# One continuous GpSimd gather stream beside seventeen stages, with a counted meeting of the other four engines

## What is computed

```python
x = x + L0_conv(group_norm(x))          # q, k, v by 1x1 and depthwise 3x3; 9 sampled points per pixel and group
t = layer_norm(tokens(x))
t = tokens(x) + t + attention(t)        # 1-D convolutions of width 3 give q, k, v; 8 heads, 4096 x 4096 softmax
t = t + mixture_of_experts(layer_norm(t))
```

## Time and profile before

| | |
|---|---|
| time, 3 runs | 9876.05, 9892.16, 9906.31 us (median 9892.16) |
| the profiled execution | 9916.45 us, its span 9914.7 us |
| mean granted TensorE clock | 0.884 |
| sampling stages | from 518.6 to 7860.9 us |
| first and last gather | 524.7 and 7385.7 us |

### The profile page before, as it was taken

One profiled execution on the slowest core, in us unless ns is written; L12 is line 12 of the kernel. 1 busy time (PEld: TensorE's weight loads), 2 busy tenths in 40 slices (PEclk: granted clock), 3 DMA queues, 4 the chain that ended last, 5 costly groups with the idle time before them and its releaser, 6 DMA issues. The chain is left out here.

```text
span 9914.7 us, 96863 instructions
## 1 busy us (share of the span) xinstructions
PE 7715.1 (78%) x31522; PEld 4163.2 (42%) x31522; DVE 5176.9 (52%) x10029; ACT 3769.7 (38%) x5495; POOL 5070.3 (51%) x4864
## 2 busy tenths in 40 slices
PE   7736665643796499977999967886999699998698
PEld 3623332443343244433444433443444344444466
DVE  6543334554565466655666645664663266644233
ACT  2101102300363166634666523562566245551222
POOL 1066776566677667776777767676750000001222
PEclk9868887876798699987999979898999899998899
DMA  3844335575553544444454454545441311106221
GB/s 127 296 138 129 120 118 159 184 233 190 155 148 104 167 130 136 133 149 131 141 147 136 124 157 153 154 136 158 138 123 40 94 31 45 47 20 172 87 71 55
DMA packets 658548, 1283.60 MB, mean 129 GB/s; under 512 B 189044, under 2 KB 398219, under 8 KB 643409
## 3 DMA queue, kind: packets, MB, share of 16 engines
q0 software_dynamic: 234240, 639.57, 21.5%
q1 hardware_dynamic: 405392, 562.58, 19.2%
q10 hardware_dynamic: 18432, 75.51, 1.9%
HBM read 1003.44 MB, written 278.91 MB: 129 GB/s over the span
## 5 line engine op out<-in xcount | busy, mean ns | idle before, releaser
L666 POOL DMA_INDIRECT sa_slot<-s_table,sa_rec x4608 | 4811.9, 1044 | 2540.8 <-issue 1374.5
L1657 DVE CUSTOM_DVE_ANT_0 a_above<-a_late,a_above 128x512 f32<-128x512 f32 x1600 | 1102.5, 689 | 1430.9 <-PE a_late L1509 1323.3
L1589 ACT ACTIVATE a_p<-a_s 128x1024 f32<-128x1024 f32 x1600 | 1628.0, 1020 | 124.0 <-PE a_s L1547 122.2
L1564 PE MATMUL a_ctx<-a_p,a_v 128*64 128x512 f32 x6400 | 1572.6, 612 | 85.1 <-issue 84.6
L1598 ACT ACTIVATE a_above<-a_diff 128x512 f32<-128x512 f32 x1600 | 957.7, 599 | 1780.9 <-PE a_diff L1497 1515.1
L713 DVE TENSOR_TENSOR sa_slot<-sa_slot,sa_q 128x1152 f32<-128x1152 f32 x512 | 694.0, 1355 | 1059.0 <-DMA sa_slot<-s_table,sa_rec 1041.4
L1547 PE MATMUL a_s<-a_q,a_k 98*128 98x512 f32 x3200 | 1047.0, 411 | 4.2 <-ACT a_p L1589 4.2
L822 PE MATMUL sa_sums<-keep_ident,sa_vals 128*128 128x128 f32 x4608 | 674.3, 295 | 453.9 <-DVE sa_vals L765 453.9
L1497 PE MATMUL a_diff<-a_kd,a_q 96*128 96x512 f32 x1600 | 724.9, 453 | 338.6 <-DMA a_q<-s_q 301.7
L1509 PE MATMUL a_late<-a_k,a_q 96*128 96x512 f32 x1600 | 816.0, 510 | 167.7 <-DVE a_pair_max L1657 166.1
L822 PEld LDWEIGHTS sa_sums<-keep_ident,sa_vals 128*128 128x128 f32 x4608 | 603.1, 154 | 551.8 <-DVE sa_vals L765 472.6
(11 more groups left out here) (280 smaller groups left out, 8093.8 us busy)
## 6 DMA issues: line engine op xcount, KB each, us to landing
sa_slot<-s_table,sa_rec POOLq DMA_INDIRECT x4608, 3.1
s_table<-t_rows ACTq DMA_DIRECT2D x64, 1024.0 KB, 8.0
a_q<-s_q SPq DMA_DIRECT2D x480, 128.0 KB, 3.5
s_part<-a_o SPq DMA_DIRECT2D x160, 256.0 KB, 2.4
t_qwin<-s_dwq SPq DMA_DIRECT2D x64, 512.0 KB
t_kvwin<-s_dwkv SPq DMA_DIRECT2D x64, 386.0 KB, 8.7
a_kd<-s_kd SPq DMA_DIRECT2D x384, 64.0 KB
a_o<-s_part SPq DMA_DIRECT2D x96, 256.0 KB, 3.3
```

The source lines that it names most:

```text
L666: pool.indirect_dma_start(out=self.slot[g][:, k, :, :, :].rearrange("p c a n -> p (c a n)"), out_offset=None, in_=self.s["table"][n // TIL ...
L1564: mm = pe.matmul(self.ps_ctx[i * 2 * HD:(i + 1) * 2 * HD, :], self.v_and_ones(run.head, kb), self.p[slot % P_SLOTS][:, i * CHUNK:(i + 1) * ...
L1589: act.activation(self.p[slot % P_SLOTS][:, :], self.ps_s[slot % 2], ACT.Exp, scale=float(HD) ** -0.5).then_inc(self.exped, 1)
L1657: dve.tensor_tensor_reduce(above, self.ps_late, above, 1.0, LOWEST, ALU.add, ALU.max, self.pair_max[:, t, j:j + 1]).then_inc(self.late_got, 1)
```

## The change

A new `Flow` opens one block around all stages with sampling. Inside it a stage is a `FlowStage`: it has no block and no barrier of its own; at its end TensorE, ScalarE, VectorE and SP drain, add 1 each to one semaphore and wait until it has reached four times the number of ended stages. SP then clears the stage's semaphores. POOL takes no part: all 4608 gathers are written as one program, limited by `tile_in`, `values_made` and the landing waits alone; before tile 32 it waits for the meeting at the end of `stage_tables_ahead`. The target rule (`freed`, the `todo` list) is gone. In `stage_maps_ahead` SP waits for each chunk of the convolution by itself and does its sampling work up to that chunk's target in between. Targets, buffers and the other engines' work are unchanged.

```diff
+class Flow(Stage):
+    ENGINES = 4
+
+    def __init__(self, nc):
+        super().__init__(nc)
+        self.met = nc.alloc_semaphore(name="flow_met")
+        self.sems.append(self.met)
+        self.block = self.enter_context(nc.Block())
+        self.ended = 0
+
+    def meeting(self):
+        return self.ENGINES * self.ended
+
+class FlowStage(ExitStack):
...
+    def meet(self):
+        flow, block = self.flow, self.flow.block
+        flow.ended += 1
+        numbers = sorted(sem.num for sem in self.sems)
+
+        @block.tensor
+        def _(pe):
+            pe.drain().then_inc(flow.met, 1)
+            pe.wait_ge(flow.met, flow.meeting())
...
+        @block.sync
+        def _(sp):
+            sp.drain().then_inc(flow.met, 1)
+            sp.wait_ge(flow.met, flow.meeting())
+            for _, same in groupby(enumerate(numbers), lambda item: item[1] - item[0]):
+                row = [number for _, number in same]
+                sp.sem_clear(range(row[0], row[-1] + 1))
+
+        for sem in self.sems:
+            self.nc.release_semaphore(sem)
...
-    def pool(self, pool, target):
-
-        todo = [j for j in range(self.done["POOL"], B * TILES * G) if self.freed(j) + HALF <= target]
-        for j in todo:
-            self.gather(pool, j // G, j % G)
-        self.done["POOL"] += len(todo)
...
+    def pool(self, pool, flow, tables_met):
+        for n in range(B * TILES):
+            if n == TILES:
+                pool.wait_ge(flow.met, tables_met)
+            for g in range(G):
+                self.gather(pool, n, g)
...
             for m in range(MT):
-                sp.wait_ge(conv_got, CHUNKS * (m + 1))
+                for c in range(CHUNKS):
+                    sp.wait_ge(conv_got, CHUNKS * m + c + 1)
+                    if c < CHUNKS - 1:
+                        sa.sync(sp, pieces(m, c))
...
-        @block.gpsimd
-        def _(pool):
-            sa.pool(pool, upto)
...
-def stage_project(nc, d, s, keep, b, c, sa, begin, upto):
+def stage_project(flow, d, s, keep, b, c, sa, begin, upto):
...
-    with Stage(nc) as stack:
+    nc, block = flow.nc, flow.block
+    with FlowStage(flow) as stack:
...
+                with Flow(nc) as flow:
+                    done = sa.stored_at(OWN_BLOCKS)
+                    stage_maps_ahead(flow, d, s, keep, 1, sa, done)
+                    for b in range(B):
+                        for c in range(QBS):
+                            if (b, c) == (0, 1):
+                                begin, done = done, sa.stored_at(2 * OWN_BLOCKS)
+                                stage_tables_ahead(flow, d, s, keep, 1, sa, begin, done)
+                                tables_met = flow.meeting()
...
+                            stage_project(flow, d, s, keep, b, c, sa, begin, done)
+                            if (b, c) < (B - 1, QBS - 1):
+                                done = stage_attention(nc, d, s, keep, b, c, row_max, sa, done, flow)
+
+                    @flow.block.gpsimd
+                    def _(pool):
+                        sa.pool(pool, flow, tables_met)
```

More of the change, by code:

```diff
@@ L1 @@
 from contextlib import ExitStack
+from itertools import groupby
 import concourse.bass as bass
@@ L76, in __exit__, with __init__, _ @@
             self.nc.all_engine_barrier()
+class Flow(Stage):
[9 more added lines that the diff above has]
+class FlowStage(ExitStack):
+    def __init__(self, flow):
+        super().__init__()
+        self.flow, self.nc, self.sems = flow, flow.nc, []
+    def __exit__(self, *error):
+        super().__exit__(*error)
+        if error[0] is None:
+            self.meet()
+    def meet(self):
[6 more added lines that the diff above has]
+            pe.wait_ge(flow.met, flow.meeting())
+        @block.scalar
+        def _(act):
+            act.drain().then_inc(flow.met, 1)
+            act.wait_ge(flow.met, flow.meeting())
+        @block.vector
+        def _(dve):
+            dve.drain().then_inc(flow.met, 1)
+            dve.wait_ge(flow.met, flow.meeting())
+        @block.sync
[7 more added lines that the diff above has]
+            self.nc.release_semaphore(sem)
 class Room:
@@ L603, in __init__ @@
         self.links = 0
-        self.done = {"SP": 0, "PE": 0, "ACT": 0, "DVE": 0, "POOL": 0}
+        self.done = {"SP": 0, "PE": 0, "ACT": 0, "DVE": 0}
     def turn(self, engine, target):
@@ L670, in gather @@
             ).then_inc(self.gathered[g] if k < EARLY else self.gathered_late[g], 16)
-    def pool(self, pool, target):
-        todo = [j for j in range(self.done["POOL"], B * TILES * G) if self.freed(j) + HALF <= target]
-        for j in todo:
-            self.gather(pool, j // G, j % G)
-        self.done["POOL"] += len(todo)
-    def freed(self, j):
-        n, g = divmod(j, G)
-        return self.PIECES * (n - 1) + HALF * (g // 4) + 11 + g % 4
+    def pool(self, pool, flow, tables_met):
[4 more added lines that the diff above has]
+                self.gather(pool, n, g)
     def vector(self, dve, target):
@@ L833, in project, with stage_maps_ahead @@
         mm.then_inc(self.projected, 1)
-def stage_maps_ahead(nc, d, s, keep, b, sa, upto):
-    with Stage(nc) as stack:
+def stage_maps_ahead(flow, d, s, keep, b, sa, upto):
+    nc, block = flow.nc, flow.block
+    with FlowStage(flow) as stack:
         r = Room(nc, stack, "n")
@@ L861, in stage_maps_ahead @@
         conv_mm, conv_got, diag_made, edges, chain, tail_zero = (r.sem(x) for x in ("conv_mm", "conv_got", "diag", "edges", "chain", "tail"))
-        block = stack.enter_context(nc.Block())
         rows = CHUNK // W
@@ L996, in _, with stage_tables_ahead @@
             sa.vector(dve, upto)
-def stage_tables_ahead(nc, d, s, keep, b, sa, begin, upto):
-    with Stage(nc) as stack:
+def stage_tables_ahead(flow, d, s, keep, b, sa, begin, upto):
+    nc, block = flow.nc, flow.block
+    with FlowStage(flow) as stack:
         ta = Tables(nc, stack, d, s, keep, b)
-        block = stack.enter_context(nc.Block())
         TURNS = TILES // 2
@@ L2391, in _, with stage_attention @@
             send(1)
-def stage_attention(nc, d, s, keep, b, c, row_max, sa, begin):
-    with Stage(nc) as stack:
+def stage_attention(nc, d, s, keep, b, c, row_max, sa, begin, flow):
+    with (FlowStage(flow) if flow else Stage(nc)) as stack:
         at = (Attention if sa else LastAttention)(nc, stack, s, keep, b, c, row_max)
         inverse = None if sa else Inverse(Room(nc, stack, "inv"), s, 0)
-        block = stack.enter_context(nc.Block())
+        block = flow.block if flow else stack.enter_context(nc.Block())
         def pieces(slot):
@@ L2419, in _ @@
             at.end_sync(sp)
[L2421 to L2424, removed]
         @block.tensor
@@ L2677, in build @@
         stage_tables(nc, d, s, keep, 0)
-        with Stage(nc) as flow:
-            row_max = Room(nc, flow, "flow").sb("row_max", [P, HEADS, QBS, QB // P])
+        with Stage(nc) as batches:
+            row_max = Room(nc, batches, "flow").sb("row_max", [P, HEADS, QBS, QB // P])
             with Stage(nc) as sampling:
                 sa = Sampling(nc, sampling, d, s, keep)
[L2682 to L2694, removed]
@@ new lines, in build @@
+                with Flow(nc) as flow:
[7 more added lines that the diff above has]
+                                tables_met = flow.meeting()
+                            begin = max(done, sa.stored_at(b * TILES + min(OWN_BLOCKS * (c + 1), TILES - 1)))
+                            done = min(begin + PROJECT_PIECES, sa.END)
+                            stage_project(flow, d, s, keep, b, c, sa, begin, done)
[4 more added lines that the diff above has]
+                        sa.pool(pool, flow, tables_met)
@@ L2695, in build @@
+            stage_attention(nc, d, s, keep, B - 1, QBS - 1, row_max, None, 0, None)
         stage_mix_route(nc, d, s, keep, out)
```

## The result

The changed kernel takes 9654.83 us (median of four runs, 9646.26 to 9666.29) against 9893.72 for the kernel before, a ratio of 0.9761 (95% interval 0.9742 to 0.9779): faster by 2.4%. The forecast was 9663. The profiled execution took 9657.97 us, 3 us over this median; the profiled one of the kernel before lay 24 us over its own.

The account below looks back on a forecast made before the run. POOL's line of 4608 gathers was taken to set the end until 6908 us, then PE's. It shortens by 36.5 + 170.5 + 40 - 18 = 229 us, giving 9663 us from 9892.16; range 9590 to 9766.

Parts of the forecast that it names:

- The bound: Up to about 6900 us POOL's and PE's lines are nearly equal; POOL's sets the end, then PE's alone.
- Records: POOL's two remaining waits for a tile's record go, since SP loads records by chunks in maps_ahead: 36.5 us.
- Barrier: POOL's standing at 15 stage borders leaves its line: 170.5 us.
- Slot waits: POOL's waits for a free slot, 80.4 us, fall by half: 40 us.
- Port: More gathers meet DVE operations at the shared SBUF port: 42 more, 0.43 us each, 18 us lost.
- Landing waits: POOL's waits for the landing of the group before, 388.2 us, stay: no change.
- The meeting: The new drain, increment and wait at seventeen borders cost as before, within 11 us either way: taken as nothing.
- The other line: PE and DVE gain over 300 us from borders, late records and gather waits, so they do not limit the gain.
- Slot-bound: Rival: POOL stands at the slot limit instead of borders, slot waits stay whole; gain 126 us, 9766; chance 0.17.
- Slower gathers: Rival: closer packing raises the mean gather to 1079 ns, costing 161 us; 9824; chance 0.08.
- The clock: Rival: PEclk falls under 0.90 in long attention stages; includes the case that the change frees nothing; chance 0.06.
- Lock-step: Rival: POOL's gathers always meet DVE's operations at the shared port; up to 809 us lost, 10472; chance 0.05.

Follow-up runs that it names:

- e10: Changed kernel with a GpSimd drain at the fifteen old borders, nobody waiting for anybody there: 9771.48 us, ratio 0.9859 to the kernel before.
- e6: Changed kernel waiting for the landing of the first 5 gathers of the group before instead of 7: 9488.05 us, ratio 0.9572 to the kernel before.
- e1: Kernel before with only SP's chunk-by-chunk work in maps_ahead added, stage barriers kept: 9885.52 us, ratio 0.9979 to the kernel before.
- e2: Changed kernel with SP again waiting for a whole channel block in maps_ahead: 9686.57 us, ratio 0.9771 to the kernel before.
- e3: Changed kernel with POOL waiting at the old borders for the other four engines, which do not wait for it: 9698.30 us, ratio 0.9793.
- e9: Changed kernel with SP at each meeting first waiting for the stage's last old-rule gather to land, POOL neither draining nor counting: 9737.29 us, ratio 0.9823.
- e4: Changed kernel with POOL draining and counting as fifth engine at old borders without waiting, the four others waiting for it: 9835.87 us, ratio 0.9922.
- e5: Changed kernel with a tighter slot limit, POOL 54 to 63 gathers ahead instead of 72: 9765.75 us, ratio 0.9856 to the kernel before.
- e8: Changed kernel with DVE's 512 products of gathered keys and q replaced by a one-input sum of the same length: 9512.82 us, ratio 0.9598.
- e11: Changed kernel waiting for the landing of the first 3 gathers of the group before instead of 7: 9461.68 us, ratio 0.9547 to the kernel before.
- e12: Changed kernel with eight gathers per group instead of nine from the second tile on, and EARLY = 3 instead of 7: 9295.32 us, ratio 0.9382.

## Why the prediction was right

**The bound** was named rightly: POOL's line up to the last sampled attention stage, which itself only shifts. e10 shows it (124 us on POOL, 97 to 117 on the total), and e6 from the other side.

**Records, 36.5 us:** gone. On the total they are worth 21 us by e1; e2's 10 us lie within the scatter.

**Barrier, 170.5 us:** gone from the line as forecast. What I had wrong is what it was. I read it as POOL waiting for the others or they for it; about 112 to 124 us were POOL's drain and restart (e10), about 48 a wait for the others (e3). The term's size was right, its make-up not seen; the drain's row stands in the profile before under another line than the waits.

**Slot waits, 40 us:** the row fell by 31.7, the waits that a slot really ended by 47 (55.4 to 8.2). Of the prediction's 80.4 us 25 were landing waits under another name, so its bound of "all gone" was too wide. The mechanism was right for the wait at 1721.56 and its like early in attention stages. "In the later, longer stages it stays" was half wrong: of two in the longest stage (11.8 and 9.6 us) one is left, with 8.2. That half of the row would go was a choice, not a derivation. What the sum did not say is that slot and landing waits are where the others' standing pays: e9 brings back 111 us of both.

**Port, -18 us:** right in kind, mis-sized, and hidden in the mean, which did not move (1044, 0.7 us in all). Counted over both traces, the gathers that start inside a two-input product or weighting rose from 955 to 985 (the prediction said 42 more), and what they take over the median from 420 to 431 us: a loss of 11 us. The median gather fell from 949 to 946 ns, 14 us over 4608, and covered it. This median lies at 946 to 949 ns in all fourteen kernels, so that part is most likely chance.

**Landing waits, 0:** the row has 35.4 us fewer, but most of this is a matter of names; by the count they fell by 11, from 415 to 404. They are 415 to 432 us in runs where the others stand for POOL (before, e1, e4, e9) and 370 to 404 where they don't (changed, e2, e3, e5, e10). A possible cause, not shown: while DVE stands, no gather is held, the group goes faster, and its last two gathers cover less of the landing. In the changed kernel groups whose last two gathers were held for 0.8 us or more wait 0.3 us on average and unheld ones 0.7, and e8, with fewer gathers held, has 436 us. But the unheld groups themselves wait less than before (0.7 us for 0.8), which this does not explain.

**The meeting, 0:** nothing speaks against it. From the last of the drains to DVE's next operation it is 0.3 to 1.2 us at the borders of both kernels (stages whose first DVE operation waits for more left out). DVE's waits there are about 30 us in all, most of them for SP.

**The other line.** I held it to have gained over 300 us where POOL's gained 229, so with some 70 to spare. It had more: e11 took 193 us off the changed kernel's time and e12 another 166, with slot waits of 120 and 602 us as the sign that the other engines now held POOL. The prediction had counted DVE's 1041 us of gather waits only in part.

**The sum.** The parts measured one by one are 97 (drains) + 32 (POOL's waits) + 61 (the others' standing) + 21 (chunks, by e1; 10 by e2) = 211 us by ratio; the whole is 239. Each part is uncertain by some 20 us, so they add as well as these runs can tell, and a remainder of 28 us stays open.

**How much was luck.** In its own terms, from one profile to the other, the forecast was 229 us and POOL's line shrank by 265, the span by 258.5. The difference of 36 us is the port's 18 that did not show and 35 of the landing row, less 8 at the slots and 8 of "issue". The medians differ by only 239 us, since the profiled execution of the kernel before was 24 us over its median and that of the changed one 3 us. That the forecast lies 8 us from the measured median is in part this accident; the mechanism and the size to within some 15% are not. The signs set beforehand: the last gather starts at 7124.8 us (forecast 7157), maps_ahead ends at 1472.9 (1464), and the landing row has 353 us (390).

**The rivals.** Slot-bound (9766): no, slot waits fell. Slower gathers: mean 1044. The clock: 0.94 and 0.95 in the long stages. Lock-step: 985 gathers held, 955 before.

## What to carry to other kernels

When one engine's instruction stream is the longest through many stages, add its idle time by cause until it closes, and take what each cause holds off the total; here that gave 229 us where the total fell by 239, with some luck in the last digits. When a wait hangs on several semaphores, look in the trace which came last before calling it by the row's name. An engine that issues DMAs should not sit in a barrier: its drain costs it several us at each one (7 to 14 here) even when nobody is waited for. And a wait on the landing of a recent transfer is a hidden floor: it is to be sized by how much work covers it, and looked at again whenever that work shrinks.

## What the runs showed that I had not expected

- A GpSimd drain behind gathers costs the engine about 8 us (e10, 124.4 us for fifteen); it starts with five to seven gathers still to end, so the drain's own row shows 12.6 to 25 us.
- Waiting for the seventh of nine gathers, rather than the third, costs 314 us of waits in 512 groups, though a landing takes 3.1 us. It was the largest single item left, and with eight gathers it grew to 1041 us.
- A DVE operation with two SBUF inputs costs a concurrent gather 0.49 us on average; a one-input operation of the same length costs nothing that shows (e8), nor does one with its second input in PSUM (517 gathers, 945 ns).
- The gain of a removed barrier appeared in the project stages (195 of 268 us), not in the attention stages, where both lines are nearly equal.
